# Whole-norm scales for two more matrices, scales and six lower halves on GpSimd, and a new order of the prologue, in a macaron block

## What is computed

```python
def ffn(x, A, B, Wr):                    # 64 experts of rank 16, 16 of them chosen
    scores = x @ Wr.T
    top_vals, top_idx = top_k(scores, 16)
    G = scatter(softmax(top_vals), top_idx)
    h = einsum('nd,krd->nkr', x, A)
    return 2.0 * einsum('nkr,kdr->nd', h * G[:, :, None], B)

def attn(x, w_gate, w_up, w_down):       # 512 -> 1376 -> 512
    s = silu(x @ w_gate.T)
    s = where(|s| is among the 688 smallest of its row, 0, s)
    return (s * (x @ w_up.T)) @ w_down.T

x = x + 0.5 * ffn(layernorm(x)); x = x + attn(layernorm(x)); x = x + 0.5 * ffn(layernorm(x))
```

## Time and profile before

| | |
|---|---|
| median of 3 runs | 715.1 us (714.95 to 715.6) |
| the profiled execution | 715.56 us, of which span 713.7 us |
| PE busy | 695.4 us, 97% of the span |
| DVE busy | 474.7 us, 67% |
| ACT busy | 360.8 us, 51% |
| POOL busy | 201.7 us, 28% |
| granted TensorE clock | 1.00 |

### The profile page before, as it was taken

One profiled execution on the slowest core, in us unless ns is written; L12 is line 12 of the kernel. 1 busy time (PEld: TensorE's weight loads), 2 busy tenths in 40 slices (PEclk: granted clock), 3 DMA queues, 4 the chain that ended last, 5 costly groups with the idle time before them and its releaser, 6 DMA issues.

```text
span 713.7 us, 10326 instructions
## 1 busy us (share of the span) xinstructions
PE 695.4 (97%) x3683; PEld 332.1 (47%) x3683; DVE 474.7 (67%) x1004; ACT 360.8 (51%) x458; POOL 201.7 (28%) x526
## 2 busy tenths in 40 slices
PE   5999999999999999999999999999999999899997
PEld 2444444545444444444445444444544444444443
DVE  4999688658586666747666575566647575638862
ACT  5867985545635254453535545253452526576220
POOL 1110334332314142240523315142331424344000
PEclk9999999999999999999999999999999999999999
DMA  9866234151734172341514334252432324123442
GB/s 332 271 166 171 75 60 86 27 102 39 137 51 95 36 109 60 85 89 41 104 30 101 74 69 88 48 89 42 98 61 51 65 44 86 31 56 71 86 89 73
DMA packets 171722, 62.27 MB, mean 87 GB/s; under 512 B 163632, under 2 KB 163632, under 8 KB 171664
## 3 DMA queue, kind: packets, MB, share of 16 engines
q1 hardware_dynamic: 171664, 61.56, 39.4%
HBM read 16.97 MB, written 4.19 MB: 30 GB/s over the span
## 4 chain that ended last, share of the span: by engine, by line
PE 80%; DVE 5%; ACT 5%; POOL 4%; issue 3%; DMA 2%; SPq 0%; DVEq 0%; POOLq 0%; ACTq 0%
PE ps L564 16%; PE ps L566 16%; PE ps L565 16%; PE ps L658 11%; PE ps L662 11%; PE ps L659 11%; ACT signs L856 3%; POOL small L493 2%; DMA mem<-w_a 1%; POOL small L490 1%; POOL small L489 1%; DVE mem L1174 1%; PE ps L585 1%; DVE w_a_lo L1079 1%; POOL small L491 1%
## 5 line engine op out<-in xcount | busy, mean ns | idle before, releaser
L856 ACT ACTIVATE signs<-mem,small 128x1376 bf16<-128x1376 f32 x112 | 161.3, 1441 | 143.2 <-POOL small L493 128.3
L658 PE MATMUL ps<-w_b_hi,pt_hi 128*128 128x512 f16 x256 | 97.0, 379 | 1.6 <-DVE x L1161 1.0
L564 PE MATMUL ps<-w_a_hi,xt_f 128*128 128x512 f16 x256 | 97.0, 379 | 1.1 <-DVE w_a_lo L1079 1.1
L659 PE MATMUL ps<-w_b_lo,pt_hi 128*128 128x512 f16 x256 | 97.0, 379 | 0.0
L566 PE MATMUL ps<-w_a_lo,xt_f 128*128 128x512 f16 x256 | 97.0, 379 | 0.0
L565 PE MATMUL ps<-w_a_hi,xt_f 128*128 128x512 f16 x256 | 97.0, 379 | 0.0
L564 PE MATMUL ps<-w_u_hi,xt 128*128 128x512 f16 (+1 forms) x192 | 68.5, 357 | 0.4 <-DVE mem L1174 0.4
L489 POOL TENSOR_SCALAR small<-small 128x1 f32<-128x1 f32 x96 | 28.4, 296 | 142.9 <-ACT signs L856 142.1
L564 PE MATMUL ps<-w_g_hi,xt 128*128 128x512 f16 (+1 forms) x192 | 68.5, 357 | 0.2 <-DVE mem L1181 0.2
L565 PE MATMUL ps<-w_g_hi,xt 128*128 128x512 f16 (+1 forms) x192 | 68.5, 357 | 0.0
L566 PE MATMUL ps<-w_g_lo,xt 128*128 128x512 f16 (+1 forms) x192 | 68.5, 357 | 0.0
(11 more groups left out here) (138 smaller groups left out, 1197.9 us busy)
## 6 DMA issues: line engine op xcount, KB each, us to landing
x<-x SPq DMA_DIRECT2D x14, 256.0 KB, 3.7
out<-x SPq DMA_DIRECT2D x14, 256.0 KB, 2.3
mem<-w_g SPq DMA_DIRECT2D x4, 688.0 KB, 12.5
mem<-w_u SPq DMA_DIRECT2D x4, 688.0 KB, 4.8
mem<-w_d SPq DMA_DIRECT2D x5, 512.0 KB, 4.7
mem<-w_a SPq DMA_DIRECT2D x4, 512.0 KB, 6.9
mem<-w_b SPq DMA_DIRECT2D x4, 512.0 KB, 9.2
pt_hi<-p_hi SPq DMA_TRANSPOSE x32, 3.2
```

Source lines behind the costliest of these rows:

```text
L564: pe.matmul(dst, x_hi, w_hi, start=start, stop=False)
L658: pe.matmul(dst, x_hi[:, c, :], hi[m.name][:, c, :], start=c == 0, stop=False)
L659: pe.matmul(dst, x_hi[:, c, :], lo[m.name][:, c, :], start=False, stop=False)
L856: act.activation(signs[:, :], mags[h], ACT.Sign, bias=thr[h], scale=-1.0, accum_out=bal[h]).then_inc(counted[h], 1)
```

## The change

- `MA` and `MU` join `WHOLE`, so a and u are normed by their whole sum of squares. For a, ACT squares the first 512 columns of a piece and DVE the other 512 (`square_right`); PE needs two one-column matmuls for each piece.
- The scale is no longer made of bits on DVE. DVE copies the norm out of PSUM (`read_norm`), POOL raises it to the power -1/2 (`make_scale`) and multiplies scales for the results (`make_inverse`), DVE takes the reciprocal (`make_unscale`). The scale is no power of two now.
- POOL makes six lower halves (`by_pool`): pieces 1 and 3 of b, g and u, each with a multiplication in place and a subtraction. `wait_low` waits on DVE's count and on POOL's.
- `experts(1, 0)` is ordered anew (`experts_begun`): for each chunk of a first the products with the upper half, one chunk later those with the lower half.
- Combine 1 uses bank `DOWN`; `read_scores` takes the copy of the scores out of `choose` and stands earlier in the first passes. `stats`, `mv` and `rvar` have two buffers for j = 1. `gates(2)` may begin when the first two banks of `ups(1)` are read, as the last tile's gates already do.
- PE's list: norms of g behind `combine(1, 0)`, a combine ahead of each of the first wide blocks, norms of d ahead of `ups(0)`, `gates(2)` ahead of `down(0)`. ACT squares all of d in one row ahead of `tanh(0)`, into `signs` and `keep`. `tile(1)` loses its own order and runs as the others do.

```diff
-    WHOLE = [MR, MB, MD]
+    WHOLE = [MR, MA, MB, MU, MD]
...
+        by_pool = [(m.name, n) for m in (MB, MG, MU) for n in (1, 3)]
...
+            def make_scale(m):
+                pool.wait_ge(norm_ready, MATS.index(m) + 1)
+                link(pool.tensor_scalar(norm_part[m.name], norm2[m.name], 2.0 ** -30, 2.0 ** -120,
+                                        ALU.mult, ALU.max))
+                pool.tensor_tensor(scale[m.name], norm_part[m.name], neg_half[:, :], ALU.pow
+                                   ).then_inc(scale_made, 1)
+            def split_lo(m, n):
+                c, k, rows = m.pieces[n]
+                pool.wait_ge(w_hi_made, pieces_before(m) + n + 1)
+                part = staged(m, c, k, rows)
+                link(pool.tensor_scalar(part, part, scale[m.name][0:rows, :], None, ALU.mult))
+                pool.tensor_tensor(lo[m.name][0:rows, c:c + k, :], part,
+                                   hi[m.name][0:rows, c:c + k, :], ALU.subtract
+                                   ).then_inc(w_lo_made_pool, 1)
...
+            def experts_begun(e, x_hi, x_lo, turn_of):
+                for c in range(DC + 1):
+                    for o in range(2):
+                        dst, cols = bank(e + o), slice(o * BANK, (o + 1) * BANK)
+                        if c < DC:
+                            pe.wait_ge(w_hi_made, pieces_before(MA) + c + 1)
+                            pe.matmul(dst, x_hi[c], hi["a"][:, c, cols], start=c == 0, stop=False)
+                            pe.matmul(dst, x_lo[c], hi["a"][:, c, cols], start=False, stop=False)
+                    if c == 1:
+                        turn(turn_of)
+                    for o in range(2):
+                        dst, cols = bank(e + o), slice(o * BANK, (o + 1) * BANK)
+                        if c:
+                            wait_low(pe, MA, c - 1)
+                            mm = pe.matmul(dst, x_hi[c - 1], lo["a"][:, c - 1, cols], start=False,
+                                           stop=c == DC)
...
             def combine(j, t, fresh=False):
                 pe.wait_ge(pt_hi_loaded, 16 * (k + 1))
-                if k == len(calls) - 2:
+                if k == 1:
+                    pe.wait_ge(x_lo_ready[1], TURNED)
+                elif k == 2:
+                    pe.wait_ge(added, 1)
+                elif k == len(calls) - 2:
...
             experts(1, 3)
+            combine(1, 0, fresh=True)
             norms(MG)
-            combine(1, 0, fresh=True)
             combine(1, 1)
...
-            def make_scale(m):
+            def read_norm(m):
                 dve.wait_ge(norm_summed, pieces_before(m) + len(m.pieces))
...
+            def square_right(n):
+                dve.scalar_tensor_tensor(out=squares(MA, n)[:, BANK:KR], in0=half, scalar=1.0,
+                                         in1=half, op0=ALU.mult, op1=ALU.mult,
+                                         accum_out=square_sums[:, at:at + 1]
+                                         ).then_inc(a_right_squared, 1)
```

More of the change, by code:

```diff
@@ L249, in squares @@
             place = {"r": signs[:, :], "a": hi["u"], "b": lo["u"], "g": hi["d"], "u": lo["d"],
-                     "d": mem[:, 2 * IPAD:4 * IPAD]}[m.name]
+                     "d": (signs, keep)[n % 2][:, :]}[m.name]
+            if m is MD:
+                return place.bitcast(BF16)[0:rows, 0:k * m.width]
             if m.name in "abgu":
@@ L269, in sum_at, with right_sum_at @@
             return sum(len(k.pieces) for k in WHOLE[:WHOLE.index(m)]) + n
+        def right_sum_at(n):
+            return sum(len(k.pieces) for k in WHOLE) + n
         def staged(m, c, n, rows):
@@ L575, in norms @@
                     if m in WHOLE:
+                        last = n == len(m.pieces) - 1
                         top = 2 * sum_at(m, n) + 1
-                        pe.matmul(bank(m.bank, 1), ones[0:rows, :],
-                                  square_tops[0:rows, top:top + 1], start=n == 0,
-                                  stop=n == len(m.pieces) - 1).then_inc(norm_summed, 1)
+                        mm = pe.matmul(bank(m.bank, 1), ones[0:rows, :],
+                                       square_tops[0:rows, top:top + 1], start=n == 0,
+                                       stop=last and m is not MA)
+                        if m is MA:
+                            pe.wait_ge(a_right_squared, n + 1)
+                            top = 2 * right_sum_at(n) + 1
+                            mm = pe.matmul(bank(m.bank, 1), ones[:, :], square_tops[:, top:top + 1],
+                                           start=False, stop=last)
+                        mm.then_inc(norm_summed, 1)
                         continue
@@ L637, in experts @@
                 if fresh:
-                    busy(4)
-                    for c in range(DC):
-                        split_done(MA, c)
-                        for o in range(2):
-                            mm = three(bank(e + o), MA, c, slice(o * BANK, (o + 1) * BANK),
-                                       x_hi[c], x_lo[c], c == 0, c == DC - 1)
+                    busy(16)
+                    mm = experts_begun(e, x_hi, x_lo, turn_of)
                 else:
@@ L914, in _ @@
             split_hi(MA, 2)
+            split_hi(MA, 3)
             turned_to_hi(1)
-            split_hi(MA, 3)
             square(MB, 0)
-            square(MB, 1)
             x_to_hi(1, 2)
+            for n in range(1, len(MB.pieces)):
+                square(MB, n)
             exps(0)
-            square(MB, 2)
-            square(MB, 3)
             square(MG, 0)
@@ L1394, in _ @@
             split_lo(MG, 0)
+            read_norm(MU)
+            p_to_lo(3)
+            x_to_lo(2, 0)
             add_ffn(1, 1)
-            x_to_lo(2, 0)
             norm_stats(2, 1)
-            split_lo(MG, 1)
-            make_scale(MU)
+            make_unscale(unscale_g, "g")
             split_lo(MG, 2)
-            split_lo(MG, 3)
-            p_to_lo(3)
+            read_scores(4)
             norm_apply(2, 1)
-            split_all(MU)
+            choose(4)
             x_to_lo(2, 1)
+            split_lo(MU, 0)
+            add_ffn(1, 2)
+            norm_stats(2, 2)
+            route(4)
+            apply_route(4)
+            split_lo(MU, 2)
             silu(0)
+            norm_apply(2, 2)
             wait_low(dve, MU, len(MU.pieces) - 1)
```

408 lines of the change are left out of this document (211 added, 197 removed).

## The result

The changed kernel takes 734.75 us (median of four, 731.05 to 736.03) against 715.08: ratio 1.027, interval 1.0241 to 1.0298, 19.7 us slower. The prediction was 712.9 us, with a range up to 716.9. The profiled execution took 736.03 us, 1.3 above the median; its span is 734.2 us.

The account below looks back on a forecast made before the run. PE bounds the kernel (97% busy), with DVE also near its limit in the prologue. Prologue gains of 7.4 us minus 5.2 us of PE waits leave 2.2: 715.1 - 2.2 = 712.9 us, range 707.3 to 716.9.

Parts of the forecast that it names:

- (1): Scale of a in the prologue: first upper half at 13.5, so ACT starts 1.2 us earlier (0.6 to 1.5).
- (2): Experts of tile 0: next tile's experts start about 21.2 instead of 23.62, a gain of 2.4 us.
- (4): Second combine uses the bank of down and no longer waits for add_ffn(1,0): a gain of 1.2 us.
- (5): The u norms ahead of tile 4's experts shrink from 12 wide to four one-column matmuls: a gain of 3.8 us.
- The price of the pair: POOL's multiply and subtraction for one lower half of 1376 columns: 3.9 us taken, bounds 2.6 to 6.5.
- slope of 3.1: Each further us in POOL's pair starts ups of tile 0 about 3.1 us later (g1, g3, u1 in a row).
- the same walk: Step through POOL, DVE and PE up to ups of tile 0: start 78.9 against 81.0, gain 7.4 - 5.2 = 2.2 us.
- Rival B: Slower by POOL's chain: a pair of 5.2 us gives 716.9, its upper bound of 6.5 gives 721; chance 0.18.
- The port: DVE and POOL share an exclusive port; whoever comes second waits for the other's whole instruction, in both directions.
- rival A: DVE does not wait for POOL, so nearly all of the 7.4 us stays: 708.1 us; chance 0.31.
- The three waits of PE: Lost at combine of tile 0 (1.5), combine of tile 3 (2.6), ups of tile 0 (1.1): 5.2 us; gates(0) 0.
- After that count 0, with up to 2 us lost: Behind ups of tile 0, gates(2) covers the later tile 0 counts: 0 lost, up to 2 us at down(0) or down(1).

Follow-up runs that it names:

- e1: Changed kernel with all six POOL lower halves given back to DVE, the rest of the change kept: 715.84 us, ratio 1.0013.
- e2: Kernel before the change, with only u's norms taken from whole sums of squares: 716.56 us, ratio 1.0016.
- e7: e2 with ACT's square of u's piece 3 moved directly behind that of piece 2: 714.43 us, ratio 0.9998.
- e10: Changed kernel without POOL's multiply in its six lower halves (wrong values): 719.3 us, ratio 1.0061.
- e13: e1 with DVE's lower halves 1 to 4 of d each waiting for POOL's search step: 712.39 us, ratio 0.9963.
- e14: e13 with d's lower half 0 waiting for the first search step and d's inverse made behind that step: 711.8 us, ratio 0.9958.
- e12: Changed kernel with idle 128-column matmuls in PE's three long waits: 732.32 us, ratio 1.0235.
- e6: e2 with 46 idle 128-column matmuls in PE's wait between u's third and fourth norm matmul: 714.72 us, ratio 0.9998.
- e4: Changed kernel with POOL's rstd(2,1) moved ahead of the lower half of g's fourth piece: 729.16 us, ratio 1.02.

## Why the prediction was wrong, point by point

**The gains (1), (2), (4), (5)** were right. The first w_a_hi starts at 13.2 (said: 13.5). Experts of tile 1 begin at 21.7 in the change and 20.2 in e1 (said: 21.2, before 23.62), the first combine at 38.4 (37.9), there is no wait in front of the second one once its bank has changed, and the u norms are four short matmuls behind a combine. Their sum, 7.4, measured as 6.8 at the experts of tile 4 in e1. That (5) needs the new place on ACT and PE is what e2 and e7 show: in the old order the wait takes it all over.

**The price of the pair** is the step that failed by most: 6.9 us instead of 3.9 (6.5 without its waits). The prediction reasoned that both operations only stream, as the memset does, and bounded the multiply at 2.2 by an affine select of 128 columns. A wide multiply with one input took 2.74 ns a column, against 0.83 for the memset. The nearest rows were not near: a memset reads nothing. The subtraction, taken at 2.55 us, costs 2.8 alone. By the prediction's own slope of 3.1 the price makes 3.0 x 3.1 = 9.3 us: with the true price the same walk gives 722.2, already slower than before and beyond the range. That slope was too flat as well: e10 took a multiply of 3.75 us out of each pair and 15.4 us off the end, 4.1 for each us. On that line, an estimate from two kernels, a pair of 3.9 would give some 724, so the forecast would have missed even with the right price. Rival B had the right mechanism and sign and the wrong upper end. The estimate from the Trainium skill ("GPSIMD Engine Reference", 3.1 Elementwise) for the subtraction, 3.0 us, is near the 2.8 measured alone. It had no bearing on the multiply, where the error lay.

**The port**: that DVE is held by POOL was right, and rival A is out; that it is always held to the end of POOL's instruction was not (w_b_lo and normed beside the multiplies of 1024 columns). Where it was held in the change's trace, DVE lost 1.0 to 3.5 us at a time.

**The three waits of PE** were at the right places but for gates(0), set at 0 because g3 would be ready at 64.3; it was ready at 75.7. They measured 4.8, 3.8, 3.5 and 0.8 us, sum 12.9, where the forecast had 5.2. With the slow matmuls behind them, ups(0) begins at 94.1 and not at 78.9, 15.2 us late; the other 7.5 of the trace's miss arise behind it.

**"After that count 0, with up to 2 us lost"** failed by 6.5 us. In e1 ups(0) begins 5.8 us ahead of the old equivalent, which would give 709.3 at the end, and e1 took 715.84. The text looked at whether gates(2) covers down(0), and not at what shares a round with the count. The pieces of d, which the new order lays between the counts, slow three rounds through the port, and tanh(1) and v wait behind the rounds: e13 gives 3.4 us of the 6.5 back. What holds the rest is not shown. In e14 holes of 1.2 ahead of down(0), 1.8 ahead of down(1) and 0.8 ahead of ups(0) are left, and no run of the new order is free of all three.

**PE's clock behind a wait** had no term. e12 prices it at 2.4 us in the change (within the spread of the two kernels) and e6 at 1.6 to 1.8 in the old order. It cannot be read off the length of a hole alone: 2.6 us in e2 and 2.7 in e1 were followed by slow matmuls, 3.6 in e4 was not.

Sum of the miss, 734.75 - 712.9 = 21.9. The runs divide it in two: the halves on POOL cost 18.9 us (e1) where the walk had 5.2, which is 13.7; and the rest of the change lost 0.7 (715.84 against 715.1) where the sum of gains promised 7.4, which is 8.1, 1.6 of it ahead of ups(0) and 6.5 behind. Of the 13.7, 9.3 are the price by the forecast's own slope and 2.4 the clock by e12; 2.0 no run divides further (the steeper slope, and the unsteady first combine, which alone moves the median by as much).

## What to carry to other kernels

Work given to an engine that shares a port comes back as waiting: DVE's busy time was 476.5 us with six lower halves fewer, and 471.6 in e1, which makes them all; and where no row shows a wide operation on an engine, the upper bound has to come from one that reads as well as writes. Behind a gain, look for the next chain of small operations that pass between engines: a one-column step of 0.3 us waited out a neighbour of 1.3 in three rounds, and shifting that neighbour by one added wait was worth 3.4 us here. A wait of PE costs its length and, in most cases here, the slow matmuls behind it; whether the second part comes through depends on the next wait.
